# ViT block on one core: VectorE reads the attention output's projection from the PSUM banks itself

## The chip, the cores and the metric

The kernel runs on one core of a Trainium2 chip. The metric is the device time of one execution in microseconds. The engines are TensorE (PE: matrix products and transposes, from SBUF into the banks of PSUM), VectorE (DVE) and ScalarE (ACT), which read and write both memories, GpSimd (POOL) and SyncE (SP), which here issues DMAs. Each engine runs its own queue in order, and they meet on semaphores.

## The reference

```python
def reference(x, tok_W, tok_b, Wq, Wk, Wv, Wproj, Wr, w1, w3, w2, s1, s3, s2):
    h = patches(x) @ tok_W + tok_b                 # 64 images, 196 tokens each, 192 wide
    h = h + attention(layernorm(h))                # 12 heads of 16, rotary q and k, causal
    h = h + moe(layernorm(h))                      # 8 experts, 2 per token, and a shared one
    return h

def attention(x):
    weights = where(causal, erf(q @ k.T / sqrt(16)) + 1, 0)
    y = weights @ v / maximum(weights.sum(-1), 1e-6)
    return y @ Wproj.T
```

The change lies in the first sum of attention and tokens, `h + y @ Wproj.T`.

## The kernel before

Three parts follow each other: attention (to about 1625 us), routing, and the feed-forward networks. Only attention is touched. It works through 32 units of two images (392 tokens, held as four tiles of up to 128 rows and 192 columns) in a software pipeline. One turn of its loop works on three units at once: the token product of a unit to come (`TOK`), normalisation and the q, k, v projections of the next unit (`LN1T`, `QK`, `VV`), the twelve pairs of heads of unit u, and for the unit before (`prev`) the transposed attention output (`YT`), the output projection (`PROJ`), the second normalisation, its transposes and the router's logits. Kinds of turn: an opening, 29 `mid` turns, and the closing ones `late`, `last` and `end`, which have no new tokens.

Each engine's code has a loop over n = 0 to 11 in which a turn's jobs are written out by hand. For a pair of heads TensorE makes the scores (L830 to L836), ScalarE copies them to `x_pair` (L420) and takes their GELU (L435), VectorE multiplies (L554), inverts (L613), weighs (L561) and masks (L569), GpSimd multiplies crosswise (L689), and TensorE multiplies with v into `y_sum` (L856 to L862), four pairs behind the scores. VectorE runs behind TensorE: the mask of pair 10 comes at VectorE's n = 11, and the attention product that needs it at TensorE's n = 2 of the next turn. Behind it stand a token product (L747) and the attention product of pair 11 at n = 3, then the transposes of `normed` (L733), which ScalarE copies to `normed_t`.

Everything that is not scores or `y_sum` goes through two banks of PSUM in turns (`NB = 2`): a job has a position, its bank is the position modulo 2, `full` counts its fillings and `free` its clearings. TensorE's `room(pos)` waits until the bank is free. `PROJ = (12, 13)`, so its halves lie in bank 0 and bank 1; the next jobs there are token products.

At n = 5 of a turn TensorE fills both `PROJ` banks from `y_t` (L797, listed as L740 in the profile: `bank<-w_proj,y_t`), each with two tiles of 192 columns. ScalarE copies each half into `h2[prev]` (through the helper `copy_out`, L411), after waiting until the stores of that buffer of two units before have gone out (`rows_out`). VectorE waits until both banks are free again (`out_of`), adds the kept tokens `h[prev]` in place (L654), and takes means and variances (`spread_of`: L533, L538, L540). The profile names both `h` and `h2` buffers `h`.

VectorE's `step` counts its instructions on one semaphore, and `settle` waits until all of them are done.

Of the kernel before, what the change touches and what calls it, by code (L numbers as in the profile page):

```python
# [17 lines left out]
ALU = mybir.AluOpType  # L18
# [10 lines left out]
D, NH, HD = 192, 12, 16  # L29
# [43 lines left out]
class Tally:  # L73
# [26 lines left out]
LN1T, QK, VV, YT, PROJ, X2T, ROUTE, TOK = (  # L100
    (1, 2), (4, 5, 6, 7), (8, 11), (9, 10), (12, 13), (16, 17), (19,), (0, 3, 14, 15))
# [13 lines left out]
NB = 2  # L115
# [16 lines left out]
def fills(kind, u, pos):  # L132

    def jobs(kind, before=99):
        return sum(1 for p in TURNS[kind] if p % NB == pos % NB and p < before)

    count = sum(jobs(k) for k in KINDS[:KINDS.index(kind)]) + jobs(kind, pos) + 1
    if kind == "mid":
        return count + (u - 1) * jobs("mid")
    return count + ((MIDS - 1) * jobs("mid") if KINDS.index(kind) > KINDS.index("mid") else 0)  # L140
# [108 lines left out]
def attention(nc, dram):  # L249


    with ExitStack() as ctx:
        def sb(name, shape, dt=F32):
            return ctx.enter_context(nc.sbuf_tensor(name, shape, dt))

        def sem(name):
            return ctx.enter_context(nc.semaphore(name))

        def ps(name):
            return ctx.enter_context(nc.psum_tensor(name, [128, 512], F32))  # L260
# [12 lines left out]
        h = [sb(f"h{s}", [128, 4, D]) for s in range(2)]  # L273
# [18 lines left out]
        h2 = [sb(f"h2_{s}", [128, 4, D]) for s in range(2)]  # L292
# [8 lines left out]
        bank = [ps(f"bank{b}") for b in range(NB)]  # L301
# [5 lines left out]
        full = [sem(f"bank_full{b}") for b in range(NB)]  # L307
        free = [sem(f"bank_free{b}") for b in range(NB)]
# [5 lines left out]
        rows_out = [sem(f"rows_out{s}") for s in range(2)]  # L314
# [80 lines left out]
        @block.scalar  # L395
        def _(act):

            act.wait_ge(zero_set, 1)
            for rows in (dram["x2"], dram["out"]):
                spare = rows[N:N + SPARE, :].rearrange("n d -> (n d)").rearrange("(p z) -> p z", p=128)  # L400
                act.dma_start(spare, zeros[:]).then_inc(zeroed, 16)
            act.dma_start(dram["table"].rearrange("(v s) c -> v (s c)", s=XU), dram["empty_table"]).then_inc(zeroed, 16)

            def turn(kind, u, prior, slot):
                prev = 1 - slot
                pairs, has_next, has_prev, has_tokens = parts_of(kind)

                def copy_out(pos, dst, rows, cols=UT):

                    act.wait_ge(full[pos % NB], fills(kind, u, pos))  # L410
                    nc.scalar.copy(dst, bank[pos % NB][0:rows, 0:cols]).then_inc(free[pos % NB], 1)  # L411

                def copy_scores(u, n, opens):

                    pair = PAIRS * u + n
                    act.wait_ge(scored, pair + 1)
                    if not opens:

                        act.wait_ge(weighted, pair - 3)
                    nc.scalar.activation(x_pair[:, n % 4], score[n % 2][:, :, 0:PACKED], ACT.Copy,  # L420
                                         scale=QK_SCALE ** -2).then_inc(copied_out, 1)

                for n in range(PAIRS):
                    if pairs and n < PAIRS - 1:
                        copy_scores(u, n + 1, kind == "first" and n < 3)
                    if n == PAIRS - 1 and has_next:
                        copy_scores(u + 1, 0, kind == "pro")
                    if pairs:

                        pair = PAIRS * u + n  # L430
                        act.wait_ge(copied_out, pair + 1)
                        if kind != "first" or n >= 4:

                            act.wait_ge(attended, pair - 3)
                        nc.scalar.activation(weights[:, n % 4], x_pair[:, n % 4], ACT.Gelu, scale=SCORE_SCALE)\  # L435
                          .then_inc(gelued, 1)
                    if n == 3 and has_next:
                        for k, pos in enumerate(LN1T):
                            copy_out(pos, normed_t[:, k * UT:(k + 1) * UT], KD)
                    if n in (2, 3, 7, 8) and has_tokens:  # L440
                        k = (2, 3, 7, 8).index(n)
                        copy_out(TOK[k], h_new[slot][:, k, :], 128, D)
                    if n in (3, 4) and has_next:
                        for t in range(2 * n - 6, 2 * n - 4):
                            copy_out(QK[t], qk_raw[:, t, :], 128, 2 * D)
                    if n in (4, 5) and has_next:
                        pos = VV[n - 4]
                        if has_prev and n == 4:

                            act.wait_ge(held_in[prev], 32 * prior + 32)  # L450
                        act.wait_ge(full[pos % NB], fills(kind, u, pos))
                        for t in range(2):
                            last = nc.scalar.copy(v[prev][:, 2 * (n - 4) + t, :, 0:HD],
                                                  bank[pos % NB][:, t * D:(t + 1) * D]
                                                  .rearrange("p (h d) -> p h d", h=NH))
                        last.then_inc(free[pos % NB], 1)
                    if n == 4 and has_prev:
                        for k, pos in enumerate(YT):
                            copy_out(pos, y_t[:, k * UT:(k + 1) * UT], KD)
                    if n == 5 and has_prev:  # L460

                        act.wait_ge(rows_out[prev], 64 * prior + 64)
                        for k, pos in enumerate(PROJ):
                            copy_out(pos, h2[prev][:, 2 * k:2 * k + 2, :].rearrange("p t d -> p (t d)"), 128, 2 * D)
                    if n in (6, 7) and has_next:
                        if kind != "pro":

                            act.wait_ge(qk_turned[n - 6][slot], 32 * turned_uses(kind, u, prior, slot, False))
                        for t in range(2 * n - 12, 2 * n - 10):

                            act.wait_ge(qk_rotated, 4 * u + 5 + t)
                            for a, parts in ((0, slice(0, 3, 2)), (1, slice(0, 2))):
                                src = rotated[:, t, a * NH:(a + 1) * NH, :].unsqueeze(2).to_broadcast([128, NH, 2, HD])
                                nc.scalar.copy(heads_of(qk[:, t], a)[:, :, parts, :], src).then_inc(qk_hi, 1)
                    if n == 8 and has_next:
                        if has_prev:

                            act.wait_ge(spread_ready, last_root(kind, u))
                        act.wait_ge(biased, u + 2)
                        nc.scalar.copy(h[prev][:], h_new[prev][:]).then_inc(h_kept, 1)  # L480
                    if n == 9 and has_prev:

                        act.wait_ge(x2t_out[prev], 16 * prior + 16)
                        for k, pos in enumerate(X2T):
                            copy_out(pos, x2_t[prev][:, k * UT:(k + 1) * UT], 128)
                    if n == 11 and has_prev:
                        act.wait_ge(logits_out[prev], 16 * prior + 16)
                        copy_out(ROUTE[0], logits[prev][:], E)

            turns(turn)  # L490
            act.wait_ge(zeroed, 48)

        @block.vector
        def _(dve):
            chain = Tally()

            def step(ins):

                chain.step(ins, vec)
# [84 lines left out]
            def turn(kind, u, prior, slot):  # L584
                prev = 1 - slot
                pairs, has_next, has_prev, has_tokens = parts_of(kind)

                def out_of(jobs):

                    for pos in jobs[-NB:]:  # L590
                        dve.wait_ge(free[pos % NB], fills(kind, u, pos))

                for n in range(PAIRS):
# [28 lines left out]
                    if n in (3, 4) and has_next:  # L622

                        shape = [128, 2 * NH, 2, HD // 2]
                        for i in range(2):
                            t = 2 * (n - 3) + i
# [7 lines left out]
                        for i in range(2):  # L634
                            t = 2 * (n - 3) + i
# [6 lines left out]
                    if n in (6, 7) and has_next:  # L642

                        for t in range(2 * n - 12, 2 * n - 10):
# [4 lines left out]
                            src = rotated[:, t].rearrange("p (a h) d -> p a h d", a=2)  # L649
                            nc.vector.tensor_tensor(lo, src, hi, ALU.subtract).then_inc(roped, 1)  # L650
                    if n == 5 and has_prev:
                        out_of(PROJ)
                        dve.wait_ge(h_kept, u)
                        step(nc.vector.tensor_tensor(h2[prev][:], h2[prev][:], h[prev][:], ALU.add))  # L654
                        spread_of(1, h2[prev])
                    if n == 6 and has_prev:
                        norm(1, last_root(kind, u), h2[prev], x2[prev], x2_ready)
# [1104 lines left out]
```

## Time and profile before

| | |
|---|---|
| median of 3 runs | 3433.06 us (3431.37 to 3438.18) |
| the profiled execution | 3431.96 us |
| its span in the profile | 3430.2 us |
| TensorE busy, matrix products | 3138.3 us (91%) |
| VectorE busy | 2433.1 us (71%) |
| ScalarE busy | 1557.6 us (45%) |
| GpSimd busy | 1373.6 us (40%) |
| mean granted clock of TensorE | 0.93 |

Times are microseconds from the start of the span. An engine's idle time stands in brackets in a timeline row, with what released it. A granted clock of 1.00 is 2.4 GHz, 0.50 is 1.2 GHz.

### The profile page before, as it was taken

The page shows a single profiled execution, that of the slowest core. Times are in us where ns is not written, and L with a number is a line of the kernel's source. Part 1 is how long each engine was busy: PE and PEld are TensorE (multiplying, and loading weights), DVE is VectorE, ACT ScalarE, POOL GpSimd, SP SyncE. Part 2 cuts the span into 40 slices and gives each one's busy share as a digit, 9 for nine tenths or more (in the row PEclk, how much of TensorE's full clock was granted, in tenths as well). Part 3 has the DMA queues.
Part 4 walks back from the last instruction along what each step waited for, and adds up shares of the span by engine and source line. Part 5 has one row for each costly group of instructions (what it writes and reads, how often), then busy time and mean ns, then how long its engine had stood idle before and what let it go on. Part 6 is the DMA issues. An engine that isn't in the chain of part 4 may idle for free. (4 is left out here: it accounts for less than half of the span.)

```text
span 3430.2 us, 72008 instructions
## 1 busy us (share of the span) xinstructions
PE 3138.3 (91%) x26164; PEld 2153.2 (63%) x26164; DVE 2433.1 (71%) x4832; ACT 1557.6 (45%) x3287; POOL 1373.6 (40%) x1170
## 2 busy tenths in 40 slices
PE   6999999999999999998129999989999999999997
PEld 5777777777777777766125555556565566566664
DVE  6999999999999999997655555555545455455543
ACT  2445444544454454543004444444555455455543
POOL 1322233223322332222205555036665565556664
PEclk9899999999999999985559999999999999999999
DMA  3333233323332333322111222234554545445443
GB/s 105 74 74 80 69 86 84 75 64 86 88 74 67 81 87 74 75 44 54 44 52 48 77 67 72 74 91 76 98 95 71 99 76 97 92 73 101 75 73 42
DMA packets 461611, 260.21 MB, mean 76 GB/s; under 512 B 339103, under 2 KB 442879, under 8 KB 457183
## 3 DMA queue, kind: packets, MB, share of 16 engines
q1 hardware_dynamic: 393632, 196.42, 24.0%
q0 software_dynamic: 54400, 49.00, 10.0%
q10 hardware_dynamic: 13262, 10.66, 0.9%
q8 instruction: 188, 3.08, 0.4%
q14 instruction: 129, 1.06, 0.1%
HBM read 107.98 MB, written 68.15 MB: 51 GB/s over the span
## 5 line engine op out<-in xcount | busy, mean ns | idle before, releaser
L1270 DVE SCALAR_TENSOR_TENSOR ffn_hidden<-ffn_up,ffn_silu 128x490 f32<-128x490 f32 (+2 forms) x534 | 350.6, 670 | 690.2 <-ACT ffn_silu L1251 653.7
L689 POOL TENSOR_TENSOR weights<-weights,x_pair 128x400 f32<-128x400 f32 x384 | 395.3, 1029 | 830.6 <-DVE weights L561 819.6
L1251 ACT ACTIVATE ffn_silu<-ffn_gate 128x490 f32<-128x490 f32 (+2 forms) x534 | 301.5, 582 | 722.8 <-PE ffn_up L1214 722.4
L1440 POOL DMA_INDIRECT out_rows<-done,ids x256 | 408.2, 1594 | 401.2 <-ACT done L1542 339.7
L613 DVE RECIPROCAL recip<-x_product 128x200 f32<-128x200 f32 x384 | 534.8, 1393 | 0.0
L1235 PE MATMUL ffn_out<-ffn_w_hi,ffn_hidden_hi 128*128 128x192 f16 (+1 forms) x2124 | 525.3, 247 | 2.2 <-DVE ffn_hidden_lo L1263 1.8
L1237 PE MATMUL ffn_out<-ffn_w_hi,ffn_hidden_lo 128*128 128x192 f16 (+1 forms) x2124 | 522.5, 246 | 0.0
L1236 PE MATMUL ffn_out<-ffn_w_lo,ffn_hidden_hi 128*128 128x192 f16 (+1 forms) x2124 | 522.5, 246 | 0.0
L747 PE MATMUL bank<-w_tok,patches 128*128 128x192 f32 x1536 | 342.8, 383 | 39.2 <-DVE minus_half L525 24.1
L1263 DVE TENSOR_TENSOR ffn_hidden_lo<-ffn_hidden,ffn_hidden_hi 128x490 f16<-128x490 f32 (+2 forms) x534 | 356.5, 668 | 16.2
L1245 ACT CAST ffn_hidden_hi<-ffn_hidden 128x490 f16<-128x490 f32 (+2 forms) x534 | 320.7, 601 | 85.7 <-DVE ffn_hidden L1270 85.7
L1429 POOL DMA_INDIRECT tokens<-dram_x,ids x256 | 281.3, 1099 | 176.9 <-DMA ids<-dram_table 90.9
L747 PEld LDWEIGHTS bank<-w_tok,patches 128*128 128x128 f32 x1536 | 300.8, 224 | 55.7 <-issue 27.8
L856 PE MATMUL y_sum<-v_held,weights 128*64 128x68 f32 (+1 forms) x1536 | 267.3, 258 | 45.3 <-DVE weights L569 45.2
L1417 POOL DMA_INDIRECT dram_table<-entry,slot_of x196 | 200.7, 1024 | 252.7 <-issue 170.7
L1235 PEld LDWEIGHTS ffn_out<-ffn_w_hi,ffn_hidden_hi 128*128 128x128 f16 (+1 forms) x2124 | 218.8, 103 | 110.2 <-issue 100.3
L420 ACT ACTIVATE x_pair<-score 128x400 f32<-128x400 f32 x384 | 192.8, 502 | 205.7 <-DVE weights L561 200.3
L435 ACT ACTIVATE weights<-x_pair 128x400 f32<-128x400 f32 x384 | 205.0, 534 | 170.3 <-PE y_sum L862 165.4
L740 PE MATMUL bank<-w_qkv,normed_t 96*128 96x192 f32 (+1 forms) x1024 | 276.6, 419 | 0.7 <-ACT normed_t L411 0.7
L858 PE MATMUL y_sum<-v,weights 128*64 128x51 f32 (+2 forms) x1536 | 252.6, 248 | 0.0
L1206 PE MATMUL ffn_gate<-ffn_tokens,ffn_w_hi 128*128 128x490 f16 (+2 forms) x534 | 198.9, 372 | 43.3 <-DVE ffn_tokens L1191 19.7
L740 PEld LDWEIGHTS bank<-w_qkv,normed_t 96*128 96x128 f32 x1024 | 182.3, 194 | 69.1 <-issue 5.1
(176 smaller groups left out, 6934.4 us busy)
## 6 DMA issues: line engine op xcount, KB each, us to landing
patches<-in_patches SPq DMA_DIRECT2D x32, 1176.0 KB, 5.3
ffn_raw<-in_w SPq DMA_DIRECT2D x18, 768.0 KB
dram_x_t<-x_t SPq DMA_DIRECT2D x32, 392.0 KB, 3.7
x_t<-dram_x_t SPq DMA_DIRECT2D x24, 512.0 KB, 5.4
base<-dram_h SPq DMA_DIRECT2D x24, 384.0 KB, 4.2
out_rows<-sums ACTq DMA_DIRECT2D x24, 384.0 KB, 4.7
v_held<-v SPq DMA_DIRECT2D x64, 102.0 KB, 2.3
dram_h<-h SPq DMA_DIRECT2D x32, 192.0 KB
```

The costliest lines, as they stand in the source:

```text
L613: nc.vector.reciprocal(recip[:, n % 2], x_product[:, n % 2]).then_inc(inverted, 1)
L689: nc.gpsimd.tensor_tensor(weights[:, n % 4], weights[:, n % 4], x_pair[:, n % 4, ::-1], ALU.mult)\
L740: last = nc.tensor.matmul(out, wide(lhs, k, t), rhs[:, k, 0:width], start=(k == 0), stop=(k == 1))
L747: last = nc.tensor.matmul(out, wide(patches[slot], i, n), tok_w[:, i, :], start=(i == 0), stop=(i == KP - 1))
L1235: nc.tensor.matmul(out, hi, w_hi[:, m, :], start=(m == 0), stop=False)
L1236: nc.tensor.matmul(out, hi, w_lo[:, m, :], start=False, stop=False)
L1237: last = nc.tensor.matmul(out, lo, w_hi[:, m, :], start=False, stop=(m == MI - 1))
L1245: nc.scalar.copy(T.hidden_hi[slot][:, m, 0:n], T.hidden[:, m % 2, 0:n]).then_inc(T.hi_ready, 1)
L1251: nc.scalar.activation(T.silu[:, m % 2, 0:n], T.gate[m % 2][:, 0:n], ACT.Silu, scale=1.0 / (TOKEN_SCALE * WEIGHT_SCALE)).then_inc(T.silued, 1)
L1263: nc.vector.tensor_tensor(T.hidden_lo[slot][:, m, 0:n], T.hidden[:, m % 2, 0:n], T.hidden_hi[slot][:, m, 0:n], ALU.subtract).then_inc(T.lo ...
L1270: nc.vector.scalar_tensor_tensor(T.hidden[:, m % 2, 0:n], T.up[m % 2][:, 0:n], HIDDEN_SCALE / (TOKEN_SCALE * WEIGHT_SCALE), T.silu[:, m % ...
L1440: nc.gpsimd.indirect_dma_start(out=dram["out"][:, :], out_offset=bass.IndirectOffsetOnAxis(ap=ids[i][0:height, t, 0:1], axis=0), in_=done[ ...
```

## The change

ScalarE no longer copies the two `PROJ` banks. VectorE waits for `rows_out`, for `h_kept` and for each bank's filling, adds bank and kept tokens straight into `h2`, half by half, and frees each bank with its add. The diff:

```diff
@@ ScalarE @@
-                    if n == 5 and has_prev:
-
-                        act.wait_ge(rows_out[prev], 64 * prior + 64)
-                        for k, pos in enumerate(PROJ):
-                            copy_out(pos, h2[prev][:, 2 * k:2 * k + 2, :].rearrange("p t d -> p (t d)"), 128, 2 * D)
@@ VectorE @@
                     if n == 5 and has_prev:
+                        dve.wait_ge(rows_out[prev], 64 * prior + 64)
+                        dve.wait_ge(h_kept, u)
+                        for k, pos in enumerate(PROJ):
+
+                            dve.wait_ge(full[pos % NB], fills(kind, u, pos))
+                            new, old = (x[prev][:, 2 * k:2 * k + 2, :].rearrange("p t d -> p (t d)") for x in (h2, h))
+                            nc.vector.tensor_tensor(new, bank[pos % NB][:, 0:2 * D], old, ALU.add)\
+                              .then_inc(free[pos % NB], 1)
                         out_of(PROJ)
-                        dve.wait_ge(h_kept, u)
-                        step(nc.vector.tensor_tensor(h2[prev][:], h2[prev][:], h[prev][:], ALU.add))
                         spread_of(1, h2[prev])
```

On VectorE, in the first turn with a unit before it, n = 5 to the start of n = 6 reads so before. `h_0` is the buffer `h2[0]`; L569 is the mask, L533 the statistics:

```order
L613 RECIPROCAL recip<-x_product 128x200 [waits weighted,multiplied_x]
L569 SCALAR_TENSOR_TENSOR weights<-weights,causal 128x2x132 [waits weighted]
L654 TENSOR_TENSOR h_0<-h_0,h 128x768 [waits h_kept,bank_free1,bank_free0]
L533 BN_STATS stats<-h_0 128x6 [waits vector_steps]
L533 BN_STATS stats<-h_0 128x6 x3
L538 BN_AGGR moments<-stats 128x2 [waits vector_steps]
```

And the same place now; the lines of the file have moved, L608 and L564 are the old L613 and L569, L528 the old L533:

```order
L608 RECIPROCAL recip<-x_product 128x200 [waits weighted,multiplied_x]
L564 SCALAR_TENSOR_TENSOR weights<-weights,causal 128x2x132 [waits weighted]
L653 TENSOR_TENSOR h_0<-bank,h 128x384 [waits bank_full0,h_kept,rows_out0]
L653 TENSOR_TENSOR h_0<-bank,h 128x384 [waits bank_full1]
L528 BN_STATS stats<-h_0 128x6 [waits vector_steps,bank_free1,bank_free0]
L528 BN_STATS stats<-h_0 128x6 x3
L533 BN_AGGR moments<-stats 128x2 [waits vector_steps]
```

One add of 768 columns has become two of 384 that wait for the banks' filling, and the waits for `bank_free` have moved behind them.

On ScalarE, n = 5 and the start of n = 6 of the same turn before:

```order
L453 COPY v<-bank 128x12x16 [waits bank_full1]
L453 COPY v<-bank 128x12x16
L411 COPY h_0<-bank 128x384 [waits bank_full0,rows_out0]
L411 COPY h_0<-bank 128x384 [waits bank_full1]
L420 ACTIVATE x_pair<-score 128x400 [waits weighted,scored]
L435 ACTIVATE weights<-x_pair 128x400 [waits attended,copied_out]
```

And now:

```order
L453 COPY v<-bank 128x12x16 [waits bank_full1]
L453 COPY v<-bank 128x12x16
L420 ACTIVATE x_pair<-score 128x400 [waits weighted,scored]
L435 ACTIVATE weights<-x_pair 128x400 [waits attended,copied_out]
```

The two copies are gone, and the copy of the next scores follows on v directly. The order of the other engines is the same.

## Rows read from the trace of the kernel before

**Rows 1.** Busy time by stretch: length, PE, PEld, DVE, ACT, POOL, clock, DMA, GB/s

```profile
170.00:1350.00 1180.00, 1124.20 (x10682) 871.04 (x10680) 1114.67 (x2473) 576.26 (x1313) 348.21 (x338) 0.94 0.33 77
```

**Rows 2.** Waits, 170 to 1500 us: total, times, longest

```profile
DVE h L654 <- issue: 40.3, 28, 2.3
...
PE y_sum L856 <- DVE weights L569: 38.0, 32, 1.5
...
PE bank L747 <- ACT normed_t L411: 13.4, 27, 1.3
```

**Rows 3.** Timeline around one add: start, duration, engine, line, what, [idle before]

```profile
614.26 2.76 PE L740 MATMUL bank<-w_proj,y_t 96*128 96x192 f32 x16
...
615.82 0.48 ACT L411 COPY h<-bank 128x384 f32<-128x384 f32 x1 [0.81 <-PE bank L740]
615.89 0.37 DVE L569 SCALAR_TENSOR_TENSOR weights<-weights,causal 128x264 f32<-128x264 f32 x1
...
617.06 0.48 ACT L411 COPY h<-bank 128x384 f32<-128x384 f32 x1 [0.77 <-PE bank L740]
...
617.63 0.96 DVE L654 TENSOR_TENSOR h<-h,h 128x768 f32<-128x768 f32 x1 [1.37 <-issue]
...
618.62 1.14 DVE L533 BATCH_NORM_STATS2 stats<-h 128x6 f32<-128x192 f32 x4
```

**Rows 4.** Timeline of VectorE, the adds alone (first, two, last mid, last)

```profile
130.39 0.96 DVE L654 TENSOR_TENSOR h<-h,h 128x768 f32<-128x768 f32 x1 [1.95 <-issue]
...
665.93 0.96 DVE L654 TENSOR_TENSOR h<-h,h 128x768 f32<-128x768 f32 x1 [1.25 <-issue]
...
715.86 0.96 DVE L654 TENSOR_TENSOR h<-h,h 128x768 f32<-128x768 f32 x1 [2.25 <-issue]
...
1492.19 0.96 DVE L654 TENSOR_TENSOR h<-h,h 128x768 f32<-128x768 f32 x1 [1.11 <-issue]
...
1618.18 0.96 DVE L654 TENSOR_TENSOR h<-h,h 128x768 f32<-128x768 f32 x1 [8.32 <-ACT h L411]
```

**Rows 5.** Timeline of TensorE and VectorE, one short turn

```profile
620.36 2.22 PE L747 MATMUL bank<-w_tok,patches 128*128 128x192 f32 x12
...
638.38 0.37 DVE L569 SCALAR_TENSOR_TENSOR weights<-weights,causal 128x264 f32<-128x264 f32 x1
...
638.81 0.38 PE L856 MATMUL y_sum<-v_held,weights 128*64 128x68 f32 x1 [1.15 <-DVE weights L569]
...
640.84 4.21 PE L747 MATMUL bank<-w_tok,patches 128*128 128x192 f32 x12
```

**Rows 6.** Busy time by stretch, in three turns (the clock is the third number from the end)

```profile
617.00:637.60 20.60, 20.60 (x255) 15.46 (x254) 19.70 (x44) 13.51 (x30) 6.55 (x7) 1.00 0.61 118
638.30:645.10 6.80, 6.29 (x34) 5.36 (x34) 6.58 (x21) 0.94 (x3) 2.07 (x2) 0.50 0.01 4
...
693.00:699.70 6.70, 6.24 (x31) 5.79 (x32) 6.63 (x15) 1.68 (x4) 2.06 (x2) 0.50 0.52 181
...
549.60:552.90 3.30, 3.30 (x12) 3.30 (x11) 3.27 (x8) 0.03 (x1) 1.03 (x1) 0.50 0.51 214
```

**Rows 7.** Timeline of TensorE, two long turns

```profile
549.07 3.76 PE L747 MATMUL bank<-w_tok,patches 128*128 128x192 f32 x12 [1.25 <-ACT normed_t L411]
...
692.31 0.27 PE L856 MATMUL y_sum<-v_held,weights 128*64 128x68 f32 x1 [1.29 <-DVE weights L569]
...
695.62 4.21 PE L747 MATMUL bank<-w_tok,patches 128*128 128x192 f32 x12 [0.46 <-ACT normed_t L411]
```

**Rows 8.** VectorE by line and form, 170 to 1500 us: busy, mean ns

```profile
L631 DVE TENSOR_TENSOR by_cos<-qk_raw,rope 128x384 f32<-128x384 f32 x110 | 60.3, 548 | 1.5 <-ACT qk_raw L411 1.5
...
L581 DVE TENSOR_TENSOR y<-y_sum,den 128x384 f32<-128x384 f32 x54 | 30.1, 557 | 1.9
```

**Rows 9.** Timeline of TensorE, the same eight projections at either clock

```profile
601.46 2.75 PE L740 MATMUL bank<-w_qkv,normed_t 96*128 96x384 f32 x8
...
1522.43 5.46 PE L740 MATMUL bank<-w_qkv,normed_t 96*128 96x384 f32 x8 [0.66 <-ACT normed_t L411]
```

## The prediction, made before the change was run

> **What bounds the kernel now.** I read the busy time by stretch first: in the attention part (170 to 1350 us) TensorE is busy 1124 us of 1180 and VectorE 1115 [rows 1]. Both are nearly full, so neither share says which of them limits, and the waits decide. In 170 to 1500 us VectorE waits 40.3 us in front of the add that the change rewrites, 28 times, and for almost nothing else. TensorE waits 38.0 us, 32 times, for VectorE's mask, line 569, ahead of the attention product at L856, and 13.4 us for ScalarE's copies of `normed_t` [rows 2]. So the two engines wait for each other once per turn, and a turn is a loop through both: add, VectorE's work up to a mask, TensorE from that attention product up to the second projection, the copy, the add.
>
> The timeline gives the loop. TensorE's projection starts at 614.26 and takes 2.76, to 617.02. ScalarE copies its first half at 615.82 and its second at 617.06, to 617.54. VectorE has finished its mask at 616.26, sits idle 1.37, adds from 617.63, starts the statistics at 618.62 [rows 3]. From there VectorE has no wait until the mask at 638.38, whose 0.37 end at 638.75; TensorE starts at 638.81 after 1.15 us of idleness [rows 5]. From 638.81 TensorE runs to the next projection.
>
> How long is a turn? By the starts of the add, 28 turns take 1492.19 - 130.39 = 1361.8, or 48.64 each [rows 4]. They are not equal. I listed all 29 starts: 21 turns take 47.9 to 48.7 ("short", mean 48.30; 617.63 to 665.93 is one), and 7 take 49.6 to 49.9 ("long", mean 49.65; 665.93 to 715.86 is one, 49.93) [rows 3, 4]. What differs is where TensorE's clock is low. In the short turn the granted clock is 0.50, that is 1.2 GHz, from 638.3 to 645.1, right behind the 1.15 us wait, and slows the token product to 4.21 us [rows 5, 6]. In the long turns the clock is still high after that first wait, so TensorE is ahead again and waits a second time for the next mask (1.29) and then for the copies of `normed_t` (1.25, or 0.46); only then does the clock fall, at 549.6 or 693, and the token product behind it takes 3.76 or 4.21 [rows 6, 7], where it takes 2.22 at the high clock [rows 5]. The first place is nearly free, since it fills what would be the second wait. The second place lies on the loop.
>
> **The change, part by part.**
> ScalarE loses two copies of 0.48 us per turn. ScalarE is not full and the copy of the scores behind them waits for TensorE, so their time on ScalarE is worth nothing by itself; if that cover were gone, it would be worth at most 0.96 us a turn. What counts is the second copy's place between projection and add.
>
> VectorE loses one add of 128x768, 0.96 us (0.99 start to start), and gains two of 128x384 [rows 3]. No VectorE add from a bank stands in the trace. Nearest is L581, which reads `y_sum` from PSUM at the same 128x384: 557 ns [rows 8]. From both sides: half of the old add, 0.48, and twice the row, 1.1. I take 0.56, since that row reads the same memory in the same shape. VectorE is free from 616.26 and the first bank is full by 615.82, so the first add ends near 616.8, inside the old idle time. Cost on the loop: none; with that idle time gone it would be 0.47 to 0.56.
>
> The second add can start when the second bank is full. ScalarE started on it at 617.06, and I give VectorE the same moment. It ends at 617.62. The order shows that the two waits for `bank_free` now stand before the statistics; I put 0.08 on them, between 0 and twice the 0.09 that lay between the end of the copy, 617.54, and the start of the old add behind three waits [rows 3]. Statistics start near 617.72 in place of 618.62: 0.90 us less on the loop per turn (bounds 0.3 with an add of 1.1 and the longer waits, and 1.1 with one of 0.48 and none).
>
> In a sentence of its own: the Trainium skill ("VectorE: DVE Perf Modes", section on the TRN2 errata) gives an instruction that reads PSUM 62 cycles of 0.96 GHz more than one that reads SBUF, an estimate of 0.06 us per add, so the gain would be 0.84 and the sum over all turns 2 us less. The row differs: 557 ns from PSUM stand against 548 for `by_cos` from SBUF at the same size [rows 8].
>
> The waits that move: VectorE's queue now stands at `rows_out` and at the banks instead of ScalarE's. `rows_out` concerns stores of two turns before, so it is met. `h_kept` was waited for already. Behind the waiting add stand the statistics, then the x_product of the next pair, as before; they all move forward. The banks are freed at about 616.8 and 617.6 against 616.3 and 617.5; the next fill of each is a token product, from 620.36 on [rows 5], so this is free, and would cost 0.5 if it were not.
>
> **The loop alone.** 31 adds lie on such a loop (28 turns, and the three closing turns; the last add, at 1618.18, waits 8.32 for the copy itself [rows 4]). 31 x 0.90 = 28 us. VectorE's own work does not stand in the way: its turn without idle time is 48.30 - 1.25 = 47.05, and becomes 47.05 - 0.99 + 0.47 + 0.56 + 0.08 = 47.2, below 48.30 - 0.90 = 47.4. TensorE's wait shrinks from 1.15 to 0.25.
>
> **Where the clock puts it back.** That wait is what stood ahead of the early fall of the clock in the short turns. With 0.25 us left of it, I expect the clock to stay high there, as it does from 617 to 637.6 with no wait at all [rows 6]. Then every turn goes the way of the long ones: TensorE does the token product in 2.22, waits 1.29 for the mask, waits for the copies, and the clock falls later, on the projections that the loop needs. In all seven long turns it fell; none was spared. A long turn less 0.90 is 48.75, against a mean of 48.64 before: +0.11. Most of the seven had a single low stretch like that of 549.6 to 552.9; the one with a double stretch, 693 to 699.7, is the turn of 49.93 [rows 6]. With all turns of this form some more will have the double one, for which I add 0.1. Sum: 28 x 0.21 = +6, less 3 x 0.90 = -3 in the closing turns: +3 us. Against the profiled execution's 3431.96 (span 3430.2) that is 3435; the median of the runs is 1.1 above that execution, so 3436.
>
> The Trainium skill ("TensorE: Matmul & The Clock Gate", section on HAM oscillation) tells of short idle moments between groups of matmuls that throw the clock back and forth. The trace agrees so far that waits of 1.2 us precede the falls; no run here shows yet what a wait of 0.25 does.
>
> **The rivals.**
> *Full gain*: the clock still falls early in most turns, because what stands ahead of it is the light run of score and attention products, and the wait only tops it up. For: in 21 of 28 turns it falls there. Against: it falls nowhere else in such products. Then 28 us go: 3405.
> *No low stretch*: the clock holds through the turn. A long turn without it saves 3.76 - 2.22 = 1.5 on the token product and, as I estimate, 0.1 behind it, 48.0; less 0.90 that is 47.1, under VectorE's 47.2, which then bounds: (48.64 - 47.2) x 28 + 3 = 43 us less, 3390. Against: seven of seven.
> *Slower*: in the long form the low stretch grows to double length and lies on product and projections. Eight projections at the low clock take 5.46 against 2.75 at the high one [rows 9]. A double stretch of some 6.8 us that covers a token product (2.0 lost) and half such a group (1.3 lost) costs 3.3, where the single stretch costs 1.6: a turn of 48.75 + 1.7 = 50.4. If this strikes half of the turns: 14 x 1.7 + 28 x 0.11 - 3 = +24, 3457. It decides from about one turn in four.
> The Trainium skill's rules for authors on that page warn only of idle gaps longer than any wait in these rows; by them no wait here would matter to the clock, which is the case of the full gain.
> *A slow add from the banks*: at 1.1 us per add the gain is 0.35 a turn; the clock argument then gives 28 x (0.21 + 0.55) - 1 = +20, 3453.
>
> **How the numbers follow.** Forecast (long form everywhere, mostly single stretches): 0.44, its own range 3424 to 3450. Full gain 0.27; no low stretch 0.07; slower by double stretches 0.18; slow add 0.04. A measurement of this kernel can tell about 0.2%, 7 us. Faster by more: 0.27 + 0.07 + 0.04 from the forecast's low end = 0.38. Slower: 0.18 + 0.03 + 0.11 from the forecast's high end = 0.32. Same: the rest, 0.30. The range leaves out the case without low stretch and the far part of the slower one: 3401 to 3457.
>
> **What would show it.** Right: the idle time before the second add under 1 us in short turns and about 1.9 in long ones; statistics 0.7 us behind the projection's end, not 1.6; an add from a bank of 0.56; TensorE's first wait per turn near 0.25, the second still near 1.3; low clock no longer right behind the first. Wrong: a first wait that stays over 0.5 (then the loop is another), adds over 0.7, or a low stretch at the old place (then the full gain comes).

## The result and the profile after

The changed kernel takes 3413.23 us (median of 4 runs, 3410.82 to 3416.46); the kernel before took 3435.62 on the same chip (3431.37 to 3441.61). The ratio is 0.9934, with a 95% interval of 0.9915 to 0.9953: 22 us less, clear of the 0.2% that a measurement can tell. The forecast was no change, 3436; the time lies inside the stated range, on the side of the rival "full gain" (3405).

The stretch of the attention part, with the columns of [rows 1], shows VectorE fuller, TensorE as before, and a higher granted clock:

```profile
170.00:1350.00 1180.00, 1122.65 (x10907) 870.35 (x10907) 1136.87 (x2543) 562.28 (x1288) 355.50 (x345) 0.96 0.34 79
```

The waits of the changed kernel from 170 to 1500 us (total, times, longest), which answer to [rows 2]:

```profile
PE bank L748 <- ACT normed_t L411: 30.8, 27, 1.3
...
PE y_sum L857 <- DVE weights L564: 27.1, 41, 3.3
...
DVE h L653 <- PE bank L741: 15.1, 27, 0.6
```

VectorE waits 15.1 us in front of its adds where it waited 40.3. TensorE waits less for masks, 27.1 in place of 38.0, and more for `normed_t`, 30.8 in place of 13.4.

Two turns on the timeline, the first one like [rows 3], the second a turn in which VectorE comes last:

```profile
464.03 2.76 PE L741 MATMUL bank<-w_proj,y_t 96*128 96x192 f32 x16
...
464.78 0.37 DVE L564 SCALAR_TENSOR_TENSOR weights<-weights,causal 128x264 f32<-128x264 f32 x1
...
465.63 0.56 DVE L653 TENSOR_TENSOR h<-bank,h 128x384 f32<-128x384 f32 x1 [0.48 <-PE bank L741]
...
466.83 0.56 DVE L653 TENSOR_TENSOR h<-bank,h 128x384 f32<-128x384 f32 x1 [0.65 <-PE bank L741]
...
467.48 1.14 DVE L528 BATCH_NORM_STATS2 stats<-h 128x6 f32<-128x192 f32 x4
...
417.88 1.01 DVE L653 TENSOR_TENSOR h<-bank,h 128x384 f32<-128x384 f32 x2
...
418.97 1.14 DVE L528 BATCH_NORM_STATS2 stats<-h 128x6 f32<-128x192 f32 x4
```

The projection ends at 466.79 and the statistics start at 467.48, 0.69 us behind it; before it was 1.60. In the second turn (417.88) the adds follow each other without idle time: there VectorE's own work sets the turn.

The starts of the statistics, first and last of 29, give the mean turn: (1470.30 - 130.70) / 28 = 47.84 us, in place of 48.64 [rows 4].

```profile
130.70 1.14 DVE L528 BATCH_NORM_STATS2 stats<-h 128x6 f32<-128x192 f32 x4
...
1470.30 1.14 DVE L528 BATCH_NORM_STATS2 stats<-h 128x6 f32<-128x192 f32 x4
```

Listed one by one, 15 of the 28 turns take 47.05 to 47.5 and 13 take 48.5 to 49.3, mostly in alternation. TensorE's rows of two neighbouring turns and the clock around them (busy time by stretch; the clock is the third number from the end), which answer to [rows 5 to 7]:

```profile
392.11 0.27 PE L857 MATMUL y_sum<-v_held,weights 128*64 128x68 f32 x1 [0.23 <-DVE weights L564]
...
393.75 3.39 PE L748 MATMUL bank<-w_tok,patches 128*128 128x192 f32 x12
...
400.62 2.22 PE L748 MATMUL bank<-w_tok,patches 128*128 128x192 f32 x12 [1.12 <-ACT normed_t L411]
...
439.16 0.27 PE L857 MATMUL y_sum<-v_held,weights 128*64 128x68 f32 x1 [0.28 <-DVE weights L564]
...
440.41 2.22 PE L748 MATMUL bank<-w_tok,patches 128*128 128x192 f32 x12
...
444.36 0.27 PE L857 MATMUL y_sum<-v_held,weights 128*64 128x68 f32 x1 [1.28 <-DVE weights L564]
...
447.67 3.73 PE L748 MATMUL bank<-w_tok,patches 128*128 128x192 f32 x12 [1.25 <-ACT normed_t L411]
```

```profile
392.80:396.00 3.20, 3.20 (x18) 2.96 (x18) 2.98 (x13) 0.33 (x1) 1.10 (x2) 0.50 0.00 0
...
418.40:447.30 28.90, 26.45 (x320) 20.17 (x318) 28.35 (x67) 15.75 (x36) 10.30 (x10) 1.00 0.50 88
447.50:450.60 3.10, 2.94 (x9) 2.94 (x10) 3.03 (x8) 0.50 (x2) 0.92 (x1) 0.50 0.83 349
```

The first wait has shrunk to 0.23 and 0.28 us; 0.22 to 0.32 in all but two of the 28 turns, with a low clock behind it or without. In the turn at 392 the clock falls right behind it all the same, for one short stretch that costs only the token product at 393.75. In the turn at 439 it holds, the waits of 1.28 and 1.25 follow, and the clock falls at 447.5 on the second token product.

Where do 22 us go to? A row that marks the start of routing, on SyncE's queue, stands at 1632.20 in the trace of before and at 1605.06 now:

```profile
1605.06 0.57 SPq L913 DMA_DIRECT2D rank<-in_rank  x1
```

So attention is 27.1 us shorter: 28 x (48.64 - 47.84) = 22.4, and 4.3 in the three closing turns (their sum is 121.7 in place of 126.0). Not all of those 4.3 us need be the change's: the later kernels with the same closing turns on TensorE and VectorE took 117.7 to 127.2 us for them. The spans differ by only 21.2. Routing took 1.7 us less, and the feed-forward part, in which no instruction has changed, took 1642.2 us in this execution and 1634.5 in that of before. Over the profiled executions of the 14 kernels here it took 1634.2 to 1645.8. For single turns and for attention I therefore read the traces, and for the whole the ratios.

### The profile page after: what moved, and what is told of

Its sections match the earlier page's. It is cut to its first block and busy times, and to the rows that moved or that the text cites. A ratio compares the mean times of both kernels' runs of the same rounds, so it can differ in the third digit from the quotient of the medians.

```text
span 3409.0 us, 71976 instructions
## 1 busy us (share of the span) xinstructions
PE 3112.3 (91%) x26164; PEld 2132.2 (63%) x26164; DVE 2435.5 (71%) x4864; ACT 1525.0 (45%) x3223; POOL 1375.0 (40%) x1170
## 5 line engine op out<-in xcount | busy, mean ns | idle before, releaser
L608 DVE RECIPROCAL recip<-x_product 128x200 f32<-128x200 f32 x384 | 534.4, 1392 | 0.0
L748 PE MATMUL bank<-w_tok,patches 128*128 128x192 f32 x1536 | 329.6, 373 | 55.9 <-ACT normed_t L411 31.9
L748 PEld LDWEIGHTS bank<-w_tok,patches 128*128 128x128 f32 x1536 | 292.8, 219 | 72.0 <-ACT normed_t L411 38.4
```

What stands on the lines that cost most here:

```text
L608: nc.vector.reciprocal(recip[:, n % 2], x_product[:, n % 2]).then_inc(inverted, 1)
L748: last = nc.tensor.matmul(out, wide(patches[slot], i, n), tok_w[:, i, :], start=(i == 0), stop=(i == KP - 1))
```

## The experiments

**Is it the path or ScalarE's load?** The first gives ScalarE its two copies back, on nobody's path:

```diff
+                    if n == 5 and has_prev:
+                        for k in range(2):
+                            nc.scalar.copy(spare_copy[:, k], h[prev][:, 2 * k:2 * k + 2, :].rearrange("p t d -> p (t d)"))
```

> The changed kernel, and ScalarE makes two copies of 128x384 from the kept tokens into a spare buffer (never read) at the place where it copied the projection's banks; nothing else waits for them. Theory path (the gain is the shorter way from the projection's end to the statistics, 0.7 us in place of 1.6): as fast as the changed kernel, 3413 us, ratio 0.993; statistics start 0.7 us behind the projection's end, turns alternate 47.1 and 48.5 us. Theory load (the gain is ScalarE's 31 x 0.96 us of copies): 3433 to 3436, ratio 1.000.

Measured: 3408.42 against 3429.04, ratio 0.9943 (0.9929 to 0.9956), like the changed kernel's 0.9934. The mean turn is 47.85. The two copies as load on ScalarE cost nothing here; the gain is on the path.

The next three take the change apart by halves. Against the changed kernel, the first of them differs so; `(1,)` is the second half, which is added from its bank. The other two have `(0,)`, the first half, and `()`, none, in both places:

```diff
@@ ScalarE @@
+                    if n == 5 and has_prev:
+
+                        act.wait_ge(rows_out[prev], 64 * prior + 64)
+                        for k, pos in enumerate(PROJ):
+                            if k not in (1,):
+                                copy_out(pos, h2[prev][:, 2 * k:2 * k + 2, :].rearrange("p t d -> p (t d)"), 128, 2 * D)
@@ VectorE @@
                         for k, pos in enumerate(PROJ):
-
-                            dve.wait_ge(full[pos % NB], fills(kind, u, pos))
                             new, old = (x[prev][:, 2 * k:2 * k + 2, :].rearrange("p t d -> p (t d)") for x in (h2, h))
-                            nc.vector.tensor_tensor(new, bank[pos % NB][:, 0:2 * D], old, ALU.add)\
-                              .then_inc(free[pos % NB], 1)
+                            if k in (1,):
+                                dve.wait_ge(full[pos % NB], fills(kind, u, pos))
+                                nc.vector.tensor_tensor(new, bank[pos % NB][:, 0:2 * D], old, ALU.add)\
+                                  .then_inc(free[pos % NB], 1)
+                            else:
+                                dve.wait_ge(free[pos % NB], fills(kind, u, pos))
+                                step(nc.vector.tensor_tensor(new, new, old, ALU.add))
                         out_of(PROJ)
```

> The kernel before, with only the second half added from its bank; the first half is still copied by ScalarE and added from SBUF. Path: the first half's copy and add lie in idle time, so the full gain, 3413 us, ratio 0.993 to 0.994. Load: half the gain, 3424, ratio 0.997.

Measured: 3407.07 against 3429.04, ratio 0.9939 (0.9925 to 0.9952): the whole gain.

> The kernel before, with only the first half added from its bank; the second half is copied by ScalarE, then added from SBUF with 384 columns in place of 768. Path: statistics start near 1.2 us behind the projection's end, 0.4 earlier than before, some 0.4 of a turn's 0.9: 3423 to 3427, ratio 0.997, if the clock's places do not change. Load: half the gain too, 3424.

Measured: 3416.96, ratio 0.9963 (0.9949 to 0.9977).

> The kernel before with both copies; only VectorE's add is split in two halves, each behind its own copy. Path: the same as with the first half direct, since the first half lies in idle time either way: 3423 to 3427, ratio 0.997. Load: no gain, 3435, ratio 1.000.

Measured: 3415.72, ratio 0.9964 (0.9950 to 0.9978). One turn of this kernel, the end of its projection and VectorE's timeline, shows why it gains without a single read from a bank: the first half is added early, and only 384 columns stand behind the second copy.

```profile
415.58 2.76 PE L750 MATMUL bank<-w_proj,y_t 96*128 96x192 f32 x16
...
417.99 0.54 DVE L663 TENSOR_TENSOR h<-h,h 128x384 f32<-128x384 f32 x1
418.89 0.56 DVE L663 TENSOR_TENSOR h<-h,h 128x384 f32<-128x384 f32 x1 [0.36 <-ACT h L411]
419.58 1.14 DVE L534 BATCH_NORM_STATS2 stats<-h 128x6 f32<-128x192 f32 x4
```

These two read alike, as the path has it and the load has not: the first half's bank does not matter. Splitting the add gives 0.36%, reading the second bank directly another 0.25% (differences of ratios). On the loop they gain less than the 0.4 us expected: the statistics start 1.30 us (first half direct) and 1.24 us (split only) behind the projection's end, in place of 1.60, so it got 0.30 and 0.36 shorter. Their mean turns are 48.15 and 48.14, 0.49 less than before. The rest comes with the clock, which their expectations had left where it was: 12 of 28 turns have a single low stretch at the early place and no other, where before it was 2.

**What does the clock do?** TensorE gets extra products into columns of `y_sum` that nobody reads, in its waits of a middle turn. The numbers are how many stand ahead of the mask of pair 10 (the first wait), of pair 11 (the second) and behind the transposes of `normed`:

```diff
+                def keep_busy(count, image):
+                    for _ in range(count):
+                        nc.tensor.matmul(y_sum[image][:, 408:512], ident[:], w_tok[:, 0:104], start=True, stop=True)
...
+                    if n == 3 and has_prev and has_tokens:
+                        keep_busy(6, 1)
+                    if n == 2 and has_prev and has_tokens:
+                        keep_busy(2, 1)
                     if n < LAG and has_prev:
                         attend("mid", u - 1, n - LAG + PAIRS, v[prev], v_held[prev])
...
+                    if n == 3 and has_prev and has_tokens:
+                        pe.wait_ge(y_ready, 2 * u - 1)
+                        keep_busy(5, 0)
```

First 0, 6 and 5 on the changed kernel:

> The changed kernel, and in each of the 29 middle turns TensorE makes 6 extra products (128x104, into unused columns of y_sum) where it waits for the mask of pair 11, and 5 where it waits for the copies of normed_t; the result does not use them. They add about 1.9 us of TensorE work per turn, in waits of 1.3 and 1.25. Theory clock (the long turns cost 48.5 against 47.1 only because the clock falls behind these two waits): the low stretches go, every turn is near VectorE's own 47.1, so 14 x 1.4 = 20 us less than the changed kernel: ratio 0.988, 3390 against 3429. Rival (the places of the low stretches follow from elsewhere, or the fill lies on the path in short turns): no gain over the changed kernel or a loss, ratio 0.993 to 0.999.

Measured: 3410.27 against 3434.08, ratio 0.9929 (0.9916 to 0.9942). Not the gain that the clock theory gave. The trace tells why: 18 of 28 turns take 47.06 to 47.4 and have no low stretch, but in the other 10 the clock falls behind the first wait, in 7 of them for a double stretch, and those take 48.3 to 49.7. One of these:

```profile
439.80 0.37 PE L866 MATMUL y_sum<-v_held,weights 128*64 128x68 f32 x1 [0.28 <-DVE weights L564]
...
441.83 4.21 PE L752 MATMUL bank<-w_tok,patches 128*128 128x192 f32 x12
...
446.55 1.61 PE L746 MATMUL y_sum<-w_tok,ident 128*128 128x104 f32 x12
```

The waits that would have taken up a late TensorE are filled now, so an early low stretch is no longer free: the fill at 446.55 lies on the path. The length of the first wait does not tell the two kinds apart: it is 0.22 to 0.38 us in all but two turns, in both kinds.

> The kernel before with the same extra products. Theory clock and loop together: without low stretches behind the waits a turn is the loop alone, a long turn less its 1.5, that is 48.0 against the mean of 48.64: ratio 0.995, 3411; and with the change on top (the other kernel) 0.9 a turn less again, so the change is worth 25 us here. If the clock still falls early behind the 1.15 us wait, which is not filled: ratio 0.999 to 1.001.

Measured: 3481.23, ratio 1.0141 (1.0125 to 1.0157), slower than either expectation. The first wait of 1.15 us stays, the clock falls behind it in all 28 turns, and a turn takes 50.1 on average. The same filling that left the time of the one kernel as it was (0.9929 against 0.9934) costs 47 us in the other.

> The changed kernel with the 6 extra products in the wait for the mask of pair 11 only. If either of the two waits is enough for the fall of the clock, the low stretch stays and the time is the changed kernel's, ratio 0.993 to 0.995; if both are needed, it is that of both filled, 0.988.

Measured: 3413.81, ratio 0.9939 (0.9924 to 0.9953).

> The changed kernel with the 5 extra products in the wait for the copies of normed_t only. The fall comes at or behind this wait in the long turns, so most of the gain is expected here if the clock theory holds: ratio 0.989 to 0.991; 0.994 if the wait for the mask is enough.

Measured: 3416.97, ratio 0.9948 (0.9934 to 0.9963). Neither wait alone decides. With the second wait filled 19 of 28 turns have a single early stretch and take 47.6 to 48.0; with the third filled 19 take 47.06 to 47.4, 6 take 49.8 and 3 lie between. So the last does not give most of the gain, as expected of it.

So the first wait had to be filled too: 1, 6, 5, then 2, 6, 5.

> The changed kernel with extra products (128x104 into unused columns of y_sum) in all three waits of a middle turn: 1 ahead of the mask of pair 10, 6 ahead of that of pair 11, 5 ahead of the token product behind normed_t. With the last two alone most turns took VectorE's 47.06 with no low stretch, and about one in four 49.7 with the clock falling just behind the first wait of 0.28 us. Theory clock (that small wait ends a run of light products and tips the clock): fewer or no such turns, mean turn 47.1 to 47.4, ratio 0.988 to 0.990. Rival (the light run before it is enough): still one turn in four, ratio 0.993.

Measured: 3396.22 against 3431.37, ratio 0.9894 (0.9879 to 0.9909). As the clock theory had it: none of the 28 turns has a low stretch, and the mean is 47.12. One product in a wait of 0.28 us is enough for that.

> The same with 2 extra products (0.35 us) in place of 1 in the first wait of 0.28. Theory clock: no low stretches; but TensorE now passes the first mask 0.1 us late, so a turn is 47.1 to 47.2 and the ratio 0.988 to 0.990. Rival: 0.993.

Measured: 3389.64, ratio 0.9884 (0.9868 to 0.9899), the lowest median here, 1.2% under the kernel before; the interval overlaps that of 1, 6, 5, and the mean turn is the same. The attention stretch, then first and last statistics of 29:

```profile
170.00:1350.00 1180.00, 1171.39 (x11680) 920.07 (x11680) 1151.09 (x2581) 567.86 (x1303) 361.37 (x350) 1.00 0.34 80
```

```profile
129.53 1.14 DVE L528 BATCH_NORM_STATS2 stats<-h 128x6 f32<-128x192 f32 x4
...
1448.85 1.14 DVE L528 BATCH_NORM_STATS2 stats<-h 128x6 f32<-128x192 f32 x4
```

The granted clock is 1.00 throughout, and the mean turn is (1448.85 - 129.53) / 28 = 47.12: VectorE's own work, with no wait in front of the adds. TensorE does more work here than in any kernel without filling.

> The kernel before with 6 extra products in its first wait of 1.15 us as well as 6 and 5 in the others. With the first wait unfilled its turns took 49.2 to 50.6. Theory loop and clock: without any low stretch a turn is the loop alone, 47.06 + 0.9 = 47.9 to 48.0, ratio 0.994 to 0.996; the difference to the changed kernel with the same filling is then the change's 0.9 us per turn and nothing else, 25 us. Rival: the clock falls in any case, 1.005 to 1.014.

Measured: 3420.19, ratio 0.9962 (0.9948 to 0.9976). First and last statistics, and one add:

```profile
136.45 1.14 DVE L533 BATCH_NORM_STATS2 stats<-h 128x6 f32<-128x192 f32 x4
...
1479.97 1.14 DVE L533 BATCH_NORM_STATS2 stats<-h 128x6 f32<-128x192 f32 x4
```

```profile
423.51 0.96 DVE L654 TENSOR_TENSOR h<-h,h 128x768 f32<-128x768 f32 x1 [0.91 <-issue]
```

The mean turn is 47.98, as expected, and nearly every one is 47.96; VectorE idles 0.91 ahead of the add and is otherwise busy. Without the clock's part the change is worth 47.98 - 47.12 = 0.86 us per turn, 24 us in 28 turns. That is all that VectorE's idle time could give: with the change it does not wait in front of its adds at all. The two kernels are 0.78% apart, 27 us (31 by the medians). Their profiled executions show what the whole adds to the 24: attention ends 38.9 us apart, 6.9 of them in the opening (first statistics at 136.45 against 129.53) and 7.8 in the closing turns. Nothing is filled there, and the changed kernel with 1, 6, 5 and that with 2, 6, 5 differ by 5.3 and 9.4 in the same two places, so these are not counted for the change.

> The changed kernel with 2 extra products in the first wait only. If the small first wait is what keeps every second turn on the early, cheap low stretch, then filling it sends all turns the long way (the step of the prediction): a turn of 48.5, mean, 0.7 more than the changed kernel, ratio 0.999. If the light products ahead of it are enough, nothing changes: 0.993 to 0.995.

Measured: 3446.39, ratio 1.0048 (1.0034 to 1.0062): slower than the kernel before and than the 0.999 expected, although the loop is as short as in the changed one.

```profile
397.90 2.22 PE L752 MATMUL bank<-w_tok,patches 128*128 128x192 f32 x12
...
401.52 0.27 PE L863 MATMUL y_sum<-v_held,weights 128*64 128x68 f32 x1 [0.96 <-DVE weights L564]
...
404.83 4.21 PE L752 MATMUL bank<-w_tok,patches 128*128 128x192 f32 x12 [1.25 <-ACT normed_t L411]
```

This is the long turn of [rows 7]. Of the 28 turns 27 are of this form here, 48.4 to 50.1 long, and 11 of them have the double stretch. The first has both waits and no low stretch, and takes 47.05. The mean is 49.08 (first and last statistics 132.36 and 1506.51).

## Why the prediction was wrong

**The loop** was right. Adds from a bank take 0.55 to 0.56 (0.56 forecast), statistics follow the projection's end by 0.69 where VectorE waits for it (0.70 forecast), the way from there to the statistics falls from 1.60 by 0.91 (0.90 forecast), the first add hides (reading the second half directly gives the whole gain), the copies as load on ScalarE cost nothing. VectorE's own turn is 47.06 to 47.12 (47.2 forecast).

The Trainium skill's page "VectorE: DVE Perf Modes" (section on the TRN2 errata) has 62 cycles more for an instruction that reads PSUM than for one that reads SBUF, by the estimate in the prediction 0.06 us. They do not show here: the mean add from a bank takes 551 ns, and the same add from SBUF, in the kernel with only the add split, 555 ns.

**The step that failed** is "With 0.25 us left of it, I expect the clock to stay high there, as it does from 617 to 637.6 with no wait at all", and what follows from it, "Then every turn goes the way of the long ones". The wait did shrink, to 0.23 to 0.28, and the clock did not stay high: in 15 of 28 turns it still fell right behind that wait. There it was mostly a single stretch (392.8 to 396.0 in the rows) where before it had mostly been the double one, it lay where TensorE has room, and the turn came out at VectorE's 47.06, by 1.2 us under the short turns of before. The other 13 took the long way, as forecast, twelve of them at 48.5 to 48.9 (48.75 forecast) and one at 49.3 with a double stretch. The mean is 47.84 where I had 48.85. The full-gain rival had the right size for attention, 28 us against 27.1 measured, but for a reason that is only half its own: the places of the low stretches did not stay as they were, their costs happened to balance, so that its number came out is in part luck.

The prediction also sorted the turns of before too neatly. Of its seven long turns two have a single low stretch at each of the two places (from 153.6 and 160.4 us, and from 1321.0 and 1327.8), so an early fall did not always spare the turn the late one.

**That the mechanism exists**, and that I only let it set in too early, is what the kernel with the first wait alone filled shows: two small products in place of 0.28 us of idleness sent 27 of 28 turns the long way, and the time went to 0.5% above the kernel before, past the forecast and towards the rival "slower" (turns near 50.0 with double stretches). My sum failed by taking 0.25 for as good as nothing. What stays open is why the clock falls behind that wait in one turn and not in the next, at the same length. The prediction's "light run" of score and attention products ahead of it is one candidate, the time since the clock last changed another; no run here varied either.

**Sizes.** The closing turns gave 4.3 us, not 2.7, but kernels with the same closing turns differ by more than that among themselves. The forecast left out that the feed-forward part varies by up to 12 us between profiled executions, which makes a sum to a few us against one execution finer than it can be tested.

The Trainium skill's page "TensorE: Matmul & The Clock Gate" tells in its section on a second HAM failure mode that short idle moments between groups of products make the clock fall and rise. The runs agree as far as waits of 0.22 to 0.32 us go: with them early falls come in 15 of 28 turns, with them filled in none. Its rule for authors (section "Why this matters for your kernels") warns only of gaps longer than any wait of a middle turn here (none is above 1.6 us), and is not enough in this case.

## What to carry to other kernels

In a pipeline where two engines wait for each other once per turn, take the gain from the loop of waits, not from busy shares: a copy on an engine with time to spare can cost its full length, and splitting the operation behind it can give much of the gain (here 0.36% of 0.61%). Where TensorE's clock falls and rises within a turn, what a shorter wait is worth depends on where the clock falls next; list the turns one by one, and expect two or three kinds of them. Test it by filling the waits, all of them, with products that nobody reads: a filling that left the first wait open cost 1.4% in one kernel here, one that filled it alone turned the gain into a loss of 0.5%.

## What the runs showed that I had not expected

A wait of 0.23 to 0.28 us matters to the clock: two products of 128x104 in its place took away the fall behind it in all turns and moved the mean turn from 47.84 to 49.08 us. Added work on the busiest engine made the kernel faster by 0.5% (0.9884 against 0.9934 of the kernel before), with the clock at 1.00 through the whole stretch. How this comes about within TensorE is not shown here; only the places of waits and falls are. One of the five executions with 1, 6 and 5 extra products took 9506 us; no trace of it is kept, nothing here explains it, and the ratio leaves it out.
